# Row maxima placed from ScalarE's queue, one Block for a normalisation and its attention, and one reordered tail in a twelve-stage decoder kernel

## What is computed

```python
x = x + L0_attn(ln(x));  x = x + L0_xattn(ln(x), ctx);  x = x + L0_ffn(ln(x))    # 16 heads of 64; 16 heads of 8, 512 keys; experts
x = x + L1_attn(ln(x));  x = x + L1_xattn(ln(x), ctx);  x = x + L1_ffn(ln(x))    # over the batch; ONE head of 128, 512 keys; token shift
x = x + L2_attn(ln(x));  x = x + L2_xattn(ln(x), ctx);  x = x + L2_ffn(ln(x))    # shifted keys; 16 heads of 8, 512 keys; int8 fake-quantised
x = x + L3_attn(ln(x));  x = x + L3_xattn(ln(x), ctx, mask);  x = x + L3_ffn(ln(x))  # both causal, 16 heads of 8, 256 keys; three low-rank blocks
```

## Time and profile before

| | |
|---|---|
| median of three runs | 1625.39 us |
| the profiled execution | 1619.48 us, of which the span is 1617.8 us |
| mean granted TensorE clock | 0.954 |
| L3 attention, from its first score product to its last sum | 1268.0 to 1386 us |
| L3 cross attention, the same | about 1430 to 1548 us |
| normalisation and wide-head attention | 728.6 to 792 us |
| tail of the quantised stage | 1220 to 1239 us |

### The profile page before, as it was taken

One profiled execution on the slowest core, in us unless ns is written; L12 is line 12 of the kernel. 1 busy time (PEld: TensorE's weight loads), 2 busy tenths in 40 slices (PEclk: granted clock), 3 DMA queues, 4 the chain that ended last, 5 costly groups with the idle time before them and its releaser, 6 DMA issues. The chain is left out here.

```text
span 1617.8 us, 30013 instructions
## 1 busy us (share of the span) xinstructions
PE 1439.9 (89%) x10746; PEld 725.6 (45%) x10746; DVE 992.2 (61%) x1940; ACT 804.3 (50%) x1498; POOL 455.9 (28%) x656
## 2 busy tenths in 40 slices
PE   7998899999999999878987899899977788978887
PEld 5777634444454443536653452222334333433354
DVE  5666488888163221364557759998376667356746
ACT  4455437677633332304541054777754456445647
POOL 7111220000003567240035430000021456134531
PEclk9999999999999999979997899999986989898999
DMA  2000263221110000001000055322000431143100
GB/s 102 1 0 0 98 203 100 54 51 30 52 69 1 1 0 0 1 1 46 18 7 1 0 161 169 100 54 50 20 13 9 167 100 50 37 167 101 51 2 27
DMA packets 82393, 85.45 MB, mean 53 GB/s; under 512 B 7244, under 2 KB 67916, under 8 KB 81772
## 3 DMA queue, kind: packets, MB, share of 16 engines
q1 hardware_dynamic: 82296, 84.18, 16.9%
HBM read 51.06 MB, written 32.51 MB: 52 GB/s over the span
## 5 line engine op out<-in xcount | busy, mean ns | idle before, releaser
L1335 ACT ACTIVATE arena<-ps 128x1024 f32<-128x1024 f32 x256 | 261.8, 1023 | 109.4 <-PE ps L1242 108.9
L1227 PE MATMUL ps<-k_stack,q_stack 49*128 49x512 bf16 x512 | 190.6, 382 | 14.5 <-DVE small L1358 12.1
L1242 PE MATMUL ps<-q_stack,k_stack 51*128 51x256 bf16 x1024 | 189.6, 272 | 0.6 <-ACT arena L1335 0.4
L1355 DVE CUSTOM_DVE_ANT_0 small<-ps,mask_b 128x512 bf16<-128x512 f32 x256 | 168.0, 689 | 29.6 <-PE ps L1227 28.1
L1358 DVE TENSOR_REDUCE small<-ps 128x1 f32<-128x512 f32 x256 | 162.0, 685 | 15.9 <-PE ps L1227 14.9
L1544 DVE TENSOR_REDUCE small<-ps 128x6 f32<-128x768 f32 x128 | 122.6, 958 | 76.3 <-PE ps L1424 73.8
L1254 PE MATMUL ps<-arena,v_pad 128*32 128x256 f32 x2048 | 162.4, 391 | 1.1 <-ACT arena L1335 1.1
L1521 ACT ACTIVATE arena<-ps 128x384 f32<-128x384 f32 x256 | 118.0, 488 | 78.4 <-PE ps L1446 77.7
L1132 POOL TENSOR_SCALAR_AFFINE_SELECT arena<-arena 128x256 f32<-128x256 f32 x256 | 101.8, 406 | 86.6 <-ACT arena L1521 86.3
L2602 DVE TENSOR_TENSOR arena<-ps,arena 128x512 f32<-128x512 f32 x64 | 44.3, 692 | 101.1 <-PE ps L2519 101.0
L2676 POOL TENSOR_TENSOR arena<-arena 128x512 f32<-128x512 f32 x64 | 79.7, 1266 | 94.3 <-ACT arena L2571 94.3
(11 more groups left out here) (357 smaller groups left out, 2983.7 us busy)
## 6 DMA issues: line engine op xcount, KB each, us to landing
q_stack<-q_scratch SPq DMA_DIRECT2D x128, 96.0 KB
k_stack<-k_scratch SPq DMA_DIRECT2D x64, 192.0 KB
k_scratch<-arena SPq DMA_DIRECT2D x8, 768.0 KB, 3.9
k_stack<-k_scratch SPq DMA_DIRECT2D x64, 96.0 KB
q_scratch<-arena SPq DMA_DIRECT2D x4, 1152.0 KB, 7.5
arena<-in_ctxT SPq DMA_DIRECT2D x8, 512.0 KB, 6.3
k_scratch<-arena SPq DMA_DIRECT2D x8, 512.0 KB, 4.7
k_scratch<-arena SPq DMA_DIRECT2D x16, 256.0 KB, 3.8
```

Of the source, the lines that this page charges most:

```text
L1227: pe.matmul(ps[:, t, :], c.q_stack[par][64 * e:64 * e + ROW_MAX, pr, t * P:(t + 1) * P], c.k_stack[par][64 * e:64 * e + ROW_MAX, pr, :], s ...
L1242: mm = pe.matmul(ps[:, bank, (ch % 2) * S:(ch % 2 + 1) * S], c.k_stack[prv][64 * e:64 * e + ROWS, pr, ch * P:(ch + 1) * P], c.q_stack[prv] ...
L1335: act.activation(buf.probs[i % 8], ps[:, bank:bank + 2, :].rearrange("p a n -> p (a n)"), ACT.Exp, scale=scale).then_inc(g["probs"].sem, 1)
L1355: dve.tensor_tensor_reduce(buf.junk[t], ps[:, t, :], c.mask_b[:, M_X + t * SC:M_X + (t + 1) * SC], 1.0, FLOOR, op0=ALU.add, op1=ALU.max, a ...
```

## The change

Three edits. (1) In the stages with 256 keys, ScalarE issues the two placement DMAs of each half batch itself, right behind its own `keep_max` copy, after a wait for that copy's signal; SyncE's list for these stages has no placements left, and the stores of k parts 1 and 2 and of q stand together ahead of the loads of batch 2. For 512 keys SyncE still places, and only the first k store and the q store change places. (2) `fetch`, `layer_norm` and `wide_head_attention` become one Block: the weights and the context of the first two batches are loaded at its start, and the copies of GpSimd and the first transposes wait for the normalised tiles that they touch. (3) In the quantised stage `lora.turn(t)` stands ahead of `down(t)` instead of behind it.

```diff
+def place_max(c, buf, eng, s, hf, par):
+    g = c.sig
+    eng.wait_ge(g["turned_out"].sem, g["turned_out"].at(s * 2 + hf + 1))
+    for e in range(2):
+        eng.dma_start(c.q_stack[par][64 * e + ROW_MAX:64 * e + ROWS, HALF * hf:HALF * hf + HALF, :],
+                      buf.maxrow[hf][8 * e:8 * e + 8, :]).then_inc(g[f"max_placed{hf}"].sem, 16)
@@ attend_transfers
+    by_sp = nk > S
     for hf in range(2):
         load(1, hf)
-    early = nk == S
-    if early:
-        place(0, 0)
     sp.wait_ge(g["parts"].sem, g["parts"].at(made.parts))
-    if early:
-        store_parts(c, sp, "k", nk, 1, 2, g["stored_k1"].sem)
-        place(0, 1)
+    store_parts(c, sp, "k", nk, 1, 2, g["stored_k1"].sem)
     store_parts(c, sp, "q", nk, 1, B // 2, g["stored_q"].sem)
...
-    for s in range(1, B + 1):
-        k = s if early else s + 1
...
+    for s in range(B + 1):
+        if 2 <= s < B:
+            load(s, 1)
+        if s and by_sp:
+            place_max(c, buf, sp, s - 1, 1, (s - 1) % 2)
+        if s in (1, 2):
+            store_parts(c, sp, "k", nk, s + 1, s + 2, g[f"stored_k{s + 1}"].sem)
+        if 1 <= s < B - 1:
             load(s + 1, 0)
-        if s < B:
-            place(s, 0)
+        if s < B and by_sp:
+            place_max(c, buf, sp, s, 0, s % 2)
@@ attend_short, scalar
                 if back and i == 3:
                     keep_max(c, buf, act, b, 1, first)
+                    place_max(c, buf, act, b, 1, 1 - par)
                 if front and i == 11:
                     keep_max(c, buf, act, s, 0, first and par == 0)
+                    place_max(c, buf, act, s, 0, par)
@@ wide_head_attention
+    norm = Norm(c, cv, mean=(4, 5, 6, 7), var=(2, 3, 2, 3), spread=(4, 5, 6, 7))
@@ sync
+            load_weights(c, sp, slot, name)
             pairs(nc, ENG.SP, body)
@@ gpsimd
+                    if isinstance(it, int):
+                        pool.wait_ge(g["ln_scaled"].sem, g["ln_scaled"].at(3 * par + 1))
@@ tensor
-            pe.wait_ge(g[f"loaded{slot}"].sem, g[f"loaded{slot}"].at(16))
...
+                    if second:
+                        pe.wait_ge(g["ln_scaled"].sem, g["ln_scaled"].at(4))
...
+            norm_pe(norm, pe)
+            pe.wait_ge(g[f"loaded{slot}"].sem, g[f"loaded{slot}"].at(16))
             steps(ENG.PE, step)
@@ quantised_ffn, tensor
         for t in range(NTI):
+            if t < NB:
+                lora.turn(pe, t, 4 + t)
             down(t)
-            if t < NTI - 1:
-                lora.turn(pe, t, 4 + t)
@@ decoder
-        fetch(c, 0, "w_l1x")
-        layer_norm(c)
-        wide_head_attention(c, 0)
+        wide_head_attention(c, 0, "w_l1x")
```

More of the change, by code:

```diff
@@ L335, in norm_dve @@
         norm.scale(dve, t)
[L338 to L357, removed]
 class FirstLoads:
@@ L1057, in load @@
         load_stacks(c, sp, b % 2, hf, b * S, b * nk, nk, b * S if key_mask else None)
[L1059 to L1064, removed]
+    by_sp = nk > S
     for hf in range(2):
         load(1, hf)
-    early = nk == S
-    if early:
-        place(0, 0)
     sp.wait_ge(g["parts"].sem, g["parts"].at(made.parts))
-    if early:
-        store_parts(c, sp, "k", nk, 1, 2, g["stored_k1"].sem)
-        place(0, 1)
+    store_parts(c, sp, "k", nk, 1, 2, g["stored_k1"].sem)
     store_parts(c, sp, "q", nk, 1, B // 2, g["stored_q"].sem)
[L1076 to L1079, removed]
-    for s in range(1, B + 1):
-        k = s if early else s + 1
-        if s > 1:
-            if s < B:
[L1084 to L1088, removed]
+    for s in range(B + 1):
[6 more added lines that the diff above has]
+        if 1 <= s < B - 1:
             load(s + 1, 0)
-        if s < B:
-            place(s, 0)
+        if s < B and by_sp:
+            place_max(c, buf, sp, s, 0, s % 2)
     for hf in range(2):
@@ L2260, in batch_attention, with wide_head_attention @@
               spread=2 * NU, residual=NU, out_proj=NU, probs=NU, max_raw=NU, summed=2 * NU, recip=NU)
-def wide_head_attention(c, slot):
+def wide_head_attention(c, slot, name):
     nc, g, ps = c.nc, c.sig, c.ps
@@ L2277, in wide_head_attention @@
     sm = c.small
-    mx, nb, sums, rec = (fold(sm[:, 4 * i:4 * i + 4], (2, 2)) for i in range(4))
+    mx, nb, sums, rec = (fold(sm[:, 32 + 4 * i:36 + 4 * i], (2, 2)) for i in range(4))
+    norm = Norm(c, cv, mean=(4, 5, 6, 7), var=(2, 3, 2, 3), spread=(4, 5, 6, 7))
     SCALE = D ** -0.5
@@ L2392, in step @@
                                        accum_out=sums[:, par, t:t + 1]).then_inc(g["probs"].sem, 1)
+            norm_act(norm, act)
+            act.wait_ge(g[f"loaded{slot}"].sem, g[f"loaded{slot}"].at(16))
             steps(ENG.Activation, step)
@@ L2421, in step @@
                            .then_inc(g["normed"].sem, 1)
+            norm_dve(norm, dve)
+            dve.wait_ge(g[f"loaded{slot}"].sem, g[f"loaded{slot}"].at(16))
             steps(ENG.DVE, step)
+    norm.advance()
     g.advance(staged=B, q_proj=B, k_proj=B, v_proj=B, q_kept=B, k_kept=B, v_kept=B, normed=2 * B, turned=2 * B,
@@ L3288, in lora_ffn @@
     return Program(sync, tensor, scalar, vector, gpsimd, advance, norm=norm)
[L3291 to L3298, removed]
 def narrow_attention(c, slot, name, ctx_keys=0, mask=None, key_mask=False, begun=False, gated=False):
```

## The result

The changed kernel takes 1692.6 us in the median (1685.8 to 1693.5), the kernel before 1624.8 beside it: ratio 1.0406, interval 1.0377 to 1.0435. It is 68 us slower, where +13.4 (1639 us) was forecast. The profiled execution has a span of 1684.1 us, against 1617.8.

What follows compares the result with a forecast made beforehand. TensorE, busy 89% of the span, was taken as the bound, so its waits decide. 40.5 - 18.4 - 6.0 - 2.7 = +13.4 us, 1639 us on the median; forecast's own range 1629 to 1652, overall 1610 to 1668.

Steps and rivals of the forecast that it cites:

- Edit 1's cost: Short attentions: ScalarE's two issues at 0.62 us delay the next exponential; 30 placements x 1.35 = 40.5 us added.
- Rival (a): ScalarE's placement issues are cheap: 0.33 us per DMA gives 1620.5 us, nothing gives 1598; chance 0.24.
- Rival (b): Short attentions: stalls halve TensorE's clock, up to 2.1 us per half batch, 63 us; half gives 1670; chance 0.11.
- Edit 1's gain: L3 and cross attention: placement stalls at step 2 and the half clock behind them go, 18.4 us saved.
- The reading of step 2: L3 attention: TensorE's 6.2 us wait arises because the placement queues behind load(2, 0), which waits for the q store.
- Rival (c): Reordering fails: load(2, 0) still late, long waits move to the stacks; some 12 of 18.4 us stay, 1651; chance 0.05.
- Edit 2: Wide head: one Block boundary, the first context wait and half-clock matmuls go; 6.0 us saved, bounds 4.5 and 6.5.
- Edit 3: Quantised tail: turn(0) moves into TensorE's 3.97 us idle time ahead of down(0); 2.7 us saved, bounds 1.5 and 5.5.
- the earlier clock that the forecast named: Quantised tail: the clock may rise earlier in the next stage's means, making the turn edit's upper bound 5.5 us.
- The signs: Trace marks: 64 issues about 0.6 us, exponentials 1.4 us later, no step 2 placement wait over 1 us, wide-head and tail timings.
- the batch of 15.3 us: Short attentions: a batch was to take 15.3 us instead of 12.7.

Runs made afterwards that it cites:

- experiment 4: Changed kernel plus eight unread 128x256 filler matmuls twice a step on TensorE, ahead of the logits of heads 4 and 12: 1653.8 us, ratio 1.0151.
- experiment 5: Changed kernel with one of each half batch's two placement DMAs issued by ScalarE, the other by SyncE at its old point: 1660.8 us, ratio 1.0208.
- experiment 7: Changed kernel with SyncE placing in the new order, and two unread copies on ScalarE where it issued its two DMAs: 1660.5 us, ratio 1.0207.
- experiment 3: Changed kernel in its new order, but SyncE issues the placements of the short attentions and ScalarE issues none: 1614.6 us, ratio 0.9931.
- experiments 6: Kernel before with the wide-head and turn edits, SyncE placing, and the short attentions' q store cut into three: 1617.0 us, ratio 0.9941.
- 8: Like the q-store-in-three kernel, but first placement ahead of stores, later stores one a step, loads waiting only for their q share: 1603.3 us, ratio 0.9887.
- experiment 10: Kernel before with only the wide head's merge into one Block: 1618.8 us, ratio 0.9958.
- experiment 1: Kernel before with the wide head in one Block and the turn ahead, without the placement change: 1617.2 us, ratio 0.996.
- 11: Kernel before with only the quantised stage's turn moved ahead of down: 1623.1 us, ratio 0.9991.
- experiment 9: Changed kernel with SyncE placing in the new order, and three unread copies on ScalarE where it issued its two DMAs: 1696.0 us, ratio 1.0438.

## Why the prediction was wrong

**Edit 1's cost, the price of one placement: nearly right.** The forecast took 0.62 us for an issue on ScalarE; it was 0.62 in the median of 64. By "Perfetto Trace Analysis" in the Trainium skill, section DMA Instruction — HWDGE, the profiled time stands in the engine's way, and the trace agrees; the 50 ns dispatch of "DMA: Bandwidth & Descriptors" in the Trainium skill, section Anatomy of one DMA, which is told of GpSimd's path, isn't what counts here. Rival (a), the cheap issue, is out. What was mis-sized is what stands around the pair: 0.29 us (0.03, 0.17 and the 0.09 of lost overlap) where I had 0.08. 30 x 1.56 = 47 us in place of 40.5: +6.5. That it all lies on the path was right: at the full clock the half batch grows by the delay (experiment 4: 1.61 for 1.56; experiments 5 and 7: 0.96 and 1.06 for 0.92 and 1.04).

**Rival (b), the clock: it was the case, and I had given it 0.11.** The step that failed is the choice between two rows: a busy share of 70% lay between 68% with a clock of 0.63 and 85% with 1.00, and the forecast took the upper one and so put the clock's cost at nothing. The busy share that I compared was moreover one of the full clock, and the same matmuls are busy longer at a lower one. Experiment 4 prices the clock at 34.9 us, of the 63 that the rival had as its most and 31.5 as its middle. A half batch at 0.50 takes 9.80 us, 1.9 more than the 7.93 of experiment 4, near the 2.1 of the rival; only some of them are there. Experiment 4 also shows that it is the idle time between the matmuls that brings the clock down: ScalarE's delay is the same there, the clock is at 1.00, and TensorE is busy 84% (6.39 of 7.64). "TensorE: Matmul & The Clock Gate" in the Trainium skill tells in its section "A second HAM failure mode: psum-queue depth-cycling" of short idle times between groups of matmuls that keep switching the clock between its levels; the trace agrees, with half batches at 0.64, 0.70 and 0.92. That rule should have raised the rival's chance.

**Edit 1's gain: 18.4 us forecast, some 8 to 12 found.** The reading of step 2 was right: its long wait is gone. What failed is the search for what is late next. I looked at load(2, 0), which was in time, and not at the placement of step 0, which the new order puts behind the stores. On SyncE (experiment 3) the gain was 0.8 us on the two stretches. With the issue on ScalarE's own queue it depends on luck: in L3 attention it is issued in the midst of the stores and ScalarE idles 8.25 us behind it (3.21 before), in the cross attention it is 0.6 us ahead of them and ScalarE idles 4.44 (3.27 before). The account of the changed kernel, by the stretches of the profiled executions: 331.6 - 257.5 = 74.1 = 47 for the delays + 34.9 for the clock - the gain; so the gain is 7.8 us. Against the forecast for edit 1: +6.5, +34.9 and 10.6 of missing gain are 52.0, and 74.1 - 22.1 is 52.0. The last term is a remainder, not a measurement of its own. Counted from the first copy to the sixth, experiment 4 has 40.9 and 37.9 us, the kernel before 38.3 and 39.6; less 1.6 us for each of eight placements that is a gain of 3.8 us in L3 attention and 8.1 in the cross attention, 11.9 in all, and the rest of the difference lies in the other parts of the stretches. That the stall is the stores' is shown by experiments 6 and 8: with the first placement behind 1.5 MB the first two intervals of L3 attention are 6.95 and 7.76 us, with it ahead of them 4.90 and 5.88.

**Rival (c)** held in its sense, that the stall stays, but not in its mechanism: the load was not late.

**Edit 2: 6.0 us forecast, 5.7 measured** in the changed kernel and in experiment 10, 7.1 between the medians. Its steps are there one by one.

**Edit 3: 2.7 us forecast, 4.25 in the changed kernel,** 2.6 in experiment 1, 3.1 in 11, with the scatter of 3 us told above. The upper value has the earlier clock that the forecast named: the next stage's first eight matmuls take 3.67 us, where they took 5.23 before.

**The signs** that were named: 64 issues of 0.62 us, yes; the exponential 1.4 us later, 1.56; the batch of 15.3 us, 18.0 in the mean, and 15.9 with fillers; no wait over 1 us at step 2, yes, but one of 5.3 at step 1, which had not been asked for; the wide head and the tail, yes.

What stays open: which half batches fall to the half clock (in the changed kernel they lie at 0.50 to 0.93 with the same delay in each), why the clock's share differs between programs of nearly the same delay (experiment 5 has 7.82 us per half batch with 0.92 of delay, experiment 7 has 7.79 with 1.04; experiment 9 has 9.14, the changed kernel 9.00), and which of the phases of some 4 us between programs are the clock's alone.

## What to carry to other kernels

Work added to an engine that feeds TensorE through a short chain costs its length plus the overlap lost on both sides, each time. If it makes TensorE idle again and again, price the clock too: here a microsecond of delay cost 1.6 to 1.8 us at each of the 30 placements, and with filler matmuls under the wait a steady half batch grew by little more than the delay. Before moving an issue ahead of another, ask of every small transfer that someone waits for within a few microseconds how many megabytes will stand ahead of it on the DMA engines, whichever queue it comes from: large stores go behind it; cutting them in pieces is not enough (experiment 6).

## What the hardware showed that I had not expected

- TensorE can be busy nearly all the time and stay at the half clock. In the half batch from 1383.10 it is busy 9.05 of 9.80 us at 0.50, and from 1376 to 1412 of the changed kernel's trace:

```profile
1376.00:1412.00 36.00, 33.07 (x276) 10.18 (x276) 12.36 (x23) 17.66 (x45) 15.47 (x42) 0.52 0.04 12
```

  Experiment 4 is busy a smaller share (84%) and is granted the full clock. A busy share read at the half clock says nothing of the share that it would take to leave it.
- Adding 128 matmuls to each of the two stages made the changed kernel 39 us faster.
- The clock makes no clean step in the loss. Over experiment 3 the two stretches lose 46 us with 0.92 us of delay, 50 with 1.04, 84 with 1.54 and 75 with 1.56 (the changed kernel): 50, 48, 55 and 48 us for each microsecond, where the bare delay of 30 placements is 30. The clock's part is there at the shortest delay that was run, and nearly in proportion.
- A transfer of 8 KB from ScalarE's queue took nearly as long as the parts of SyncE's q store issued beside it: from 1266.39 to 1273.12, 6.7 us, against 2.0 in the steady steps. "DMA: Bandwidth & Descriptors" in the Trainium skill, section "Issuing engines are not separate DMA queues", says that DMAs of all engines run on the same 16 DMA engines and interleave; the trace agrees that another queue is no way around a full one.
